# Doublings of the state tables with both parts of a complex number in one instruction

## What is computed

```python
A  = -exp(log_A_real) + 1j * A_imag          # (128 channels, 64 states)
dtA = exp(log_dt)[:, None] * A
Ct = (C_re + 1j * C_im) * (exp(dtA) - 1) / A
V  = exp(dtA[:, :, None] * arange(1024))
K  = 2 * real(einsum('hn,hnl->hl', Ct, V))   # (128, 1024)
y  = irfft(rfft(x, 2048) * rfft(K, 2048))[:1024]
...
gate_logits = xn @ Wg.T; top 2 of 8 experts; softmax over the two
out = sum of gate * (silu(xn @ W1) * (xn @ W2)) @ W3
```

## Time and profile before

| | |
|---|---|
| time of three runs | 861.29 us median (860.84, 861.29, 863.75) |
| profiled execution | span 820.2 us; its own time is not listed apart, and 41.1 us lie between its span and the median of the runs |
| PE busy | 757.8 us (92%), 3893 matmuls |
| DVE busy | 658.9 us (80%) |
| ACT busy | 550.4 us (67%) |
| POOL busy | 146.5 us (18%), 138 instructions |
| 45.9 to 97.8 us of the span | DVE busy 50.2 of 51.9 us, PE 23.7 us, POOL 41.2 us |
| 150 to 820 us of the span | PE busy 658.5 of 670.0 us |

### The profile page before, as it was taken

The page is one execution under the profiler, slowest core; times in us unless marked ns, Lnnn a source line. Parts: engine busy times, 40 slices in busy tenths (PEclk is TensorE's granted clock), DMA queues, the critical chain, the costliest instruction groups (busy, mean ns, idle before and its releaser), DMA issues.

```text
span 820.2 us, 11626 instructions
## 1 busy us (share of the span) xinstructions
PE 757.8 (92%) x3893; PEld 615.2 (75%) x3893; DVE 658.9 (80%) x1558; ACT 550.4 (67%) x939; POOL 146.5 (18%) x138
## 2 busy tenths in 40 slices
PE   6956366999999998999999999999999999999998
PEld 6624255888888645868788878887888887999997
DVE  7699767899937689998799889976777778877775
ACT  5833123344434368898999899889999997665663
POOL 0067775000000254643044000000000000000000
PEclk9978659899999999999999999999999999999999
DMA  8834582689876512413033112211211210000000
GB/s 251 347 104 137 185 285 90 200 250 289 291 223 195 163 40 70 86 54 89 15 102 81 40 38 59 47 43 44 55 45 49 52 27 0 14 14 20 14 20 27
DMA packets 81274, 85.15 MB, mean 104 GB/s; under 512 B 7361, under 2 KB 59841, under 8 KB 80961
## 3 DMA queue, kind: packets, MB, share of 16 engines
q1 hardware_dynamic: 77120, 76.04, 31.3%
q0 software_dynamic: 4096, 8.40, 3.5%
HBM read 59.12 MB, written 25.30 MB: 103 GB/s over the span
## 4 chain that ended last, share of the span: by engine, by line
PE 75%; POOL 9%; DVE 8%; issue 4%; ACT 3%; DMA 1%; SPq 0%; DVEq 0%; POOLq 0%
PE ps L1829 19%; PE ps L1831 18%; PE ps L1830 18%; POOL x_slots L643 9%; PE ps L1948 6%; PE ps L2024 3%; PE ps L2171 3%; DVE hid_lo L1755 2%; PE ps L1842 1%; PE ps L1927 1%; PE ps L2198 1%; PE ps L1869 1%; PE ps L1848 1%; DVE xn L1436 1%; ACT L880 1%
## 5 line engine op out<-in xcount | busy, mean ns | idle before, releaser
L1755 DVE TENSOR_TENSOR hid_lo<-hid,hid_hi 128x512 fp32r<-128x512 f32 x256 | 175.3, 686 | 52.1 <-ACT hid_hi L881 49.5
L880 ACT ACTIVATE hid<-ps,b_sb 128x512 f32<-128x512 f32 x256 | 177.7, 694 | 36.7 <-PE ps L1831 18.8
L881 ACT ACTIVATE hid_hi<-ps,b_sb 128x512 fp32r<-128x512 f32 x256 | 176.0, 688 | 0.0
L1829 PE MATMUL ps<-hid_hi,w_lo 128*128 128x512 f32 x256 | 102.1, 399 | 5.4 <-DVE hid_lo L1755 5.2
L1829 PE MATMUL ps<-xt_hi,w_lo 128*128 128x512 f32 x256 | 102.4, 400 | 1.5 <-DVE xn L1428 1.5
L1831 PE MATMUL ps<-xt_hi,w_hi 128*128 128x512 f32 x256 | 99.9, 390 | 0.0
L1831 PE MATMUL ps<-hid_hi,w_hi 128*128 128x512 f32 x256 | 99.8, 390 | 0.0
L1830 PE MATMUL ps<-xt_lo,w_hi 128*128 128x512 f32 x256 | 99.8, 390 | 0.0
L1830 PE MATMUL ps<-hid_lo,w_hi 128*128 128x512 f32 x256 | 99.8, 390 | 0.0
L792 ACT ACTIVATE act<-ps 128x512 f32<-128x512 f32 (+1 forms) x57 | 34.0, 596 | 81.6 <-PE ps L1831 81.6
L643 POOL DMA_INDIRECT x_slots<-xn,slot x64 | 71.4, 1115 | 62.6 <-DVE expert_of L1158 43.4
(11 more groups left out here) (337 smaller groups left out, 1543.9 us busy)
## 6 DMA issues: line engine op xcount, KB each, us to landing
gate_row<-gates_dram SPq DMA_DIRECT2D x64, 256.0 KB, 4.8
wc<-w_split SPq DMA_DIRECT2D x57, 256.0 KB, 3.7
w_split<-wc SPq DMA_DIRECT2D x8, 768.0 KB, 4.1
x_slots<-prod SPq DMA_DIRECT2D x11, 512.0 KB, 9.7
xc<-x_slots SPq DMA_DIRECT2D x19, 256.0 KB, 4.3
y_slots<-yo SPq DMA_DIRECT2D x19, 256.0 KB, 4.1
wst<-w SPq DMA_DIRECT2D x16, 256.0 KB, 4.7
wd<-w SPq DMA_DIRECT2D x19, 192.0 KB, 3.1
```

The source lines that it names most:

```text
L880: nc.scalar.activation(hid1[:, u % 4], ps[:, u % 4], ACT.Gelu_apprx_tanh, bias=b1_sb[:, u:u + 1])
L881: nc.scalar.activation(hid1_hi[:, u % 4], ps[:, u % 4], ACT.Gelu_apprx_tanh, bias=b1_sb[:, u:u + 1]).then_inc(hid1_done, 1)
L1755: tt(hid1_lo[:, u % 4], hid1[:, u % 4], hid1_hi[:, u % 4].bitcast(F32), sub).then_inc(hid1_lo_done, 1)
L1829: mm(dst, a_lo, b_hi, start=first, stop=False)
```

## The change

Both parts of a complex number are handled in one instruction. The tables' first axis (real, imaginary) becomes part of the shape, so that `here * cosine` is one product of twice the columns, and `here * sines` another, where `sines` takes planes 4 and 6 of `base`, plus and minus the sine (for `high` the other way round, by the negative lags of `turn_lags`). The sum adds the two products crossed: its second input walks the part axis backwards (`at + 3:at + 1:-1`), so that one `add` gives both parts. A level has 6 instructions of 64 x 2^n columns instead of 12 of 32 x 2^n; level 0 is done for `low` as well, instead of two copies. `base_powers` writes the product with the sine to plane 4 and its negative to plane 6. `consts` grows by the ten numbers of `turn_lags`.

```diff
--- before.py
+++ after.py
@@ -137,11 +137,12 @@
         rstd = tmp("rstd", [P, G * B])
         shift0 = tmp("shift0", [P, G * B])
         newton = tmp("newton", [P, G * B])
-        consts = tmp("consts", [P, LO + NB + E + E * E])
+        consts = tmp("consts", [P, LO + 2 * NB + E + E * E])
         count_up = consts[:, 0:LO]
         base_lags = consts[:, LO:LO + NB]
-        rev = consts[:, LO + NB:LO + NB + E]
-        upto = consts[:, LO + NB + E:].rearrange("p (e f) -> p e f", e=E)
+        turn_lags = consts[:, LO + NB:LO + 2 * NB]
+        rev = consts[:, LO + 2 * NB:LO + 2 * NB + E]
+        upto = consts[:, LO + 2 * NB + E:].rearrange("p (e f) -> p e f", e=E)
         wg0_sb = tmp("wg0_sb", [P, E])
         small = tmp("small", [P, 4, HH])
         ks = tmp("ks", [P, 24, HH])
@@ -1181,10 +1182,10 @@
 
                 k = lambda i: base[:, i]
                 col = lambda a: a.unsqueeze(1).broadcast_to((P, NB, HH))
-                lag = base_lags.unsqueeze(2).broadcast_to((P, NB, HH))
+                lag, turn = (a.unsqueeze(2).broadcast_to((P, NB, HH)) for a in (base_lags, turn_lags))
                 tt(k(3), col(AR), lag, mul).then_inc(decay_done, 1)
-                v1 = step.mark(tt(k(0), col(FH), lag, mul))
-                v2 = step.mark(tt(k(2), col(FL), lag, mul))
+                v1 = step.mark(tt(k(0), col(FH), turn, mul))
+                v2 = step.mark(tt(k(2), col(FL), turn, mul))
                 need(v1)
                 v1 = step.mark(ts(k(1), k(0), MAGIC, MAGIC, add, sub))
                 need(v1)
@@ -1201,50 +1202,39 @@
                 k = lambda i: base[:, i]
                 dve.wait_ge(base_done, 4)
                 v1 = step.mark(ts(k(1), k(5), -2.0, 1.0, mul, add))
-                step.mark(tt(k(6), k(3), k(4), mul))
+                v2 = step.mark(tt(k(4), k(3), k(4), mul))
                 need(v1)
-                v1 = step.mark(tt(k(5), k(3), k(1), mul))
-                need(v1)
+                step.mark(tt(k(5), k(3), k(1), mul))
+                need(v2)
+                v2 = step.mark(ts(k(6), k(4), -1.0, None, mul))
+                need(v2)
 
             def doublings(d):
 
                 hs = slice(d * HC, (d + 1) * HC)
-                re, im, g0, g1 = low[:, 0, hs], low[:, 1, hs], high[:, 0, hs], high[:, 1, hs]
+                tables = ((low, 0, 0), (high, NB // 2, 4))
+                step.mark(nc.vector.memset(low[:, 0, hs, 0:1], 1.0))
+                step.mark(nc.vector.memset(low[:, 1, hs, 0:1], 0.0))
+                step.mark(nc.vector.tensor_copy(high[:, 0, hs, 0:1], CTR[:, hs].unsqueeze(2)))
+                v = step.mark(ts(high[:, 1, hs, 0:1], CTI[:, hs].unsqueeze(2), -1.0, None, mul))
                 for n in range(5):
                     a, b_ = slice(0, 1 << n), slice(1 << n, 2 << n)
-                    wide_ = lambda i, v: base[:, v, i, hs].unsqueeze(2).broadcast_to((P, HC, 1 << n))
-                    tmp_ = lambda i: half_way[:, i, :, a]
-                    c, s = wide_(n, 5), wide_(n, 6)
-                    if n == 0:
-                        step.mark(nc.vector.memset(re[:, :, a], 1.0))
-                        step.mark(nc.vector.memset(im[:, :, a], 0.0))
-                        step.mark(nc.vector.tensor_copy(re[:, :, b_], c))
-                        step.mark(nc.vector.tensor_copy(im[:, :, b_], s))
-                        step.mark(nc.vector.tensor_copy(g0[:, :, a], CTR[:, hs].unsqueeze(2)))
-                        v = step.mark(ts(g1[:, :, a], CTI[:, hs].unsqueeze(2), -1.0, None, mul))
+                    need(v)
+                    ready = []
+                    for table, lag_, at in tables:
+                        here = table[:, :, hs, a]
+                        cosine = base[:, 5, lag_ + n, hs].unsqueeze(1).unsqueeze(3).broadcast_to((P, 2, HC, 1 << n))
+                        sines = base[:, 4:7:2, lag_ + n, hs].unsqueeze(3).broadcast_to((P, 2, HC, 1 << n))
+                        step.mark(tt(half_way[:, at:at + 2, :, a], here, cosine, mul))
+                        ready.append(step.mark(tt(half_way[:, at + 2:at + 4, :, a], here, sines, mul)))
+                    for (table, lag_, at), v in zip(tables, ready):
                         need(v)
-                    else:
-                        step.mark(tt(tmp_(0), re[:, :, a], c, mul))
-                        step.mark(tt(tmp_(1), im[:, :, a], s, mul))
-                        step.mark(tt(tmp_(2), re[:, :, a], s, mul))
-                        v_low = step.mark(tt(tmp_(3), im[:, :, a], c, mul))
-                    c, s = wide_(n + 5, 5), wide_(n + 5, 6)
-                    step.mark(tt(tmp_(4), g0[:, :, a], c, mul))
-                    step.mark(tt(tmp_(5), g1[:, :, a], s, mul))
-                    step.mark(tt(tmp_(6), g1[:, :, a], c, mul))
-                    v_high = step.mark(tt(tmp_(7), g0[:, :, a], s, mul))
-                    if n:
-                        need(v_low)
-                        step.mark(tt(re[:, :, b_], tmp_(0), tmp_(1), sub))
-                        step.mark(tt(im[:, :, b_], tmp_(2), tmp_(3), add))
-                    need(v_high)
-                    v = step.mark(tt(g0[:, :, b_], tmp_(4), tmp_(5), add))
-                    if n < 4:
-                        v = step.mark(tt(g1[:, :, b_], tmp_(6), tmp_(7), sub))
-                        need(v)
-                    else:
-                        need(v)
-                        tt(g1[:, :, b_], tmp_(6), tmp_(7), sub).then_inc(tables_done, 1)
+                        crossed = half_way[:, at + 3:at + 1:-1, :, a]
+                        op = tt(table[:, :, hs, b_], half_way[:, at:at + 2, :, a], crossed, add)
+                        if table is high and n == 4:
+                            op.then_inc(tables_done, 1)
+                        else:
+                            v = step.mark(op)
 
             angles()
             w0_low(0)
@@ -2242,6 +2232,7 @@
     dft = np.stack([np.cos(angle), -np.sin(angle)]).astype(np.float32)
     fwd = dft.reshape(2, CT, P, HF).transpose(2, 1, 0, 3)
     inv = dft.transpose(0, 2, 1).reshape(2, HM, P, C).transpose(2, 1, 0, 3)
+    lags = 2 ** np.array([1, 2, 3, 4, 5, 8, 0, 9, 6, 7])
     tile, expert = np.divmod(np.arange(T * E), E)
     earlier = (tile[:, None] < tile) & (expert[:, None] == expert)
     prefix = np.concatenate([earlier, expert[:, None] == np.arange(E)], 1).astype(np.float32)
@@ -2256,7 +2247,7 @@
             np.concatenate([a["L0_ffn_W3"].transpose(0, 2, 1), np.broadcast_to(a["L0_attn_ln_b"], (E, 1, H)),
                             np.zeros((E, J0 * P - HID0 - 1, H), np.float32)], 1)
             .reshape(E, J0, P, P).transpose(0, 2, 1, 3).reshape(E, P, J0 * P)], 2),
-        lag_row=np.concatenate([np.arange(LO), 2 ** np.array([1, 2, 3, 4, 5, 8, 0, 9, 6, 7]), E - np.arange(E), np.tril(np.ones((E, E))).ravel()]).astype(np.float32),
+        lag_row=np.concatenate([np.arange(LO), lags, np.where(np.arange(NB) < NB // 2, lags, -lags), E - np.arange(E), np.tril(np.ones((E, E))).ravel()]).astype(np.float32),
         prefix=prefix.reshape(2, P, T * E + E).transpose(1, 0, 2),
         dft_fwd=fwd, dft_inv=inv,
         wqk_t=np.stack([a["L1_attn_W_query"].T, a["L1_attn_W_key"].T], 1),
```

## The result

The changed kernel took 851.07 us in the median of four runs (849.2 to 851.92), the kernel before 861.15 beside it: a ratio of 0.9847, 95% interval 0.981 to 0.9884, so some 10 us or 1.5% faster. The forecast was 864.3, within 861.8 to 866.4.

What follows compares the result with a forecast made beforehand. PE's start of chunk 1 was taken as bound by the later of two paths: DVE, 3.6 us earlier, and scatters, last one 4.7 us later. Net +3.0 us on 861.3 gave 864.3 us, range 861.8 to 866.4.

Steps and rivals of the forecast that it cites:

- Net 3.6 us earlier: DVE's doublings: fewer instructions, less one added scaling, end 3.6 us earlier (3.0 to 4.0).
- I take nothing: DVE's crossed sums: the backward step of the second input costs no extra time per column.
- its rival: DVE's crossed sums are slow: up to 8 us more, 866 to 869 us in all; chance 0.05.
- Scatters are held longer: POOL's scatters beside wider DVE instructions: holds of 9.2 us instead of 5.3, last scatter 4.7 us later.
- 1.0 us: Last doubling level: a scatter waits this long for a 1024-column DVE instruction's end, twice in each half.
- the first rival: Longer DVE instructions do not hold scatters longer: 859.6 us, or 857.7 if scatters were even freed; chance 0.10.
- the 0.6 on entering the last level: POOL's scatters: 0.6 us of hold in each half where the doublings' last level begins.
- the spectra's products: DVE products of 512 columns beside the last half dozen scatters: 0 to 1.7 us more hold, 0.8 taken.
- the runs' median stands 41.1 above the span, so 861.3 + 3.0: Whole kernel: 41.1 us added to the forecast span of 823.2 us, giving 864.3 us.
- two paths meet at the start of chunk 1's up products: PE's start at 144.46 awaits the later of the scatter path (142.80) and the DVE path, 1.66 us later.
- not named: Something unnamed in DMA traffic that comes 3.6 us earlier, either side; chance 0.05.
- the case that I described: Chunk 1's up products: DVE path ends at 140.9, scatter path at 147.5, so PE starts 3.0 us later.

Runs made afterwards that it cites:

- a_again: The changed kernel run and profiled again with no edit: 849.09 us, ratio 0.986 to the kernel before.
- b_again: The kernel before run and profiled again with no edit: 861.24 us, profiled span 863.4 us.
- after: The changed kernel as first measured and profiled: 851.07 us, profiled span 847.4 us.
- a_spaced: The changed kernel with a POOL memset of 256 columns ahead of each scatter from scatter 20 on: 840.87 us.
- b_spaced: The kernel before with a POOL memset of 256 columns ahead of each scatter from scatter 20 on: 840.5 us.
- b_hold: The kernel before with a POOL memset of 256 columns ahead of every second scatter from 8 to 30: 856.38 us.
- the pads: The changed kernel with unused products behind each half of the doublings: three of 512 columns (856.97 us) or one (857.13 us).
- a_lead: The changed kernel with one of two products of the last level left out: 854.22 us.
- b_lead: The kernel before with three of eight products of the last level left out in each half: 861.6 us.

## Why the prediction was wrong

**"Net 3.6 us earlier" on DVE: right in kind, 0.7 too much.** The subtraction of the fifth expert came 2.92 us earlier. Halves of the doublings last 15.62 and 15.63 us instead of 17.31 and 17.25, the scaling costs 0.39. Levels 1, 2 and 4 saved what was counted; level 0 saved nothing (1.47 us for 1.43, where I had 1.29), for its instructions of 64 columns start 0.17 apart, not 0.13 as those of level 1 in the earlier trace rows; and level 3 saved 0.30, where 0.42 was counted. "I take nothing" for the backward step was right, so its rival fell.

**Scatters are held longer: right; their sum and their tail were mis-sized.** They took 1.96 us beside 1024 columns, twice in each half, where 0.96 and "1.0 us" of waiting were worked out. The Trainium skill's rule that the shared read interface is held for the whole instruction (SBUF — State Buffer, Who interferes with whom) agrees with this, the remark on the same page that tensor_tensor did not stall such DMAs doesn't, and with it the first rival fell. But the holds in the two halves came to 7.4 us (scatters 10 to 34), not 9.2: beside the level of 512 columns, where 0.9 was counted for each half, 0.1 and 0.4 came, and the 0.6 on entering the last level came in one half only. Scatter 35 came 2.1 us later, not 3.9 (3.5 in `a_again` against `b_again`, both from their first scatter), and the last one 1.2, not 4.7 (2.2 in that pair). From scatter 38 on all of the changed kernel's take 0.96 us, where four of before take 1.29 to 1.55: the spectra's products, counted with 0.8 more, came only after the last scatter.

**The sum: its base failed.** The step that failed first is "the runs' median stands 41.1 above the span, so 861.3 + 3.0": it took 41.1 as a constant around the span. In `b_again` the profiled execution took 865.25 us with a span of 863.4, so that term is 2 us; the time of the execution shown is not on record. The others lie within the span of usual executions and were absent from the one shown: 32.5 ahead of chunk 1's up products (144.46 to 176.95) and 10.8 behind them (675.7 to 686.5). That "two paths meet at the start of chunk 1's up products" was true of an execution like none of the runs on record (the fastest of before took 845.98, this one's span is 820.2). In the others the stalled stretch decides which of PE's steps wait: in `after` chunk 1's up products start at 162.85, 18.4 us later than in the execution shown and 14.1 earlier than in `b_again`. There what I booked as the cost, scatters held longer, goes with the gain. What was "not named" had 0.05.

**Where its mechanism holds.** With the stretch all but closed, `a_spaced` against `b_spaced` is the case that I described: DVE's subtraction 2.5 us earlier (93.55 for 96.09), the last scatter 2.3 later, and chunk 1's up products with it, 2.4 later (157.64 for 155.27), not +3.0. The medians differ by 0.4 us. There the change is worth nothing; its 10 to 12 us are what it takes off the stretch, and a memset ahead of each scatter takes off more.

**Open.** Shown is that the stretch needs scatters under way, ends in a pause of theirs, opens earliest where they were held least ahead of it, and hardly opens with POOL instructions between them. What in the chip stalls, why in steps of 0.70 us, and what tips it over at a given moment, no run shows. Full DMA engines are not what keeps it up: their share is 0.29 from 120 to 130 us of the changed kernel, against 0.79 in the 10 us before. That the change gains by its hold is argued from the order of the runs and not shown, for no run holds scatters without parting them or moving DVE. Nor does hold alone explain the changed kernel: `b_hold` and the pads delay scatter 36 as much (102.5 to 102.7), and stay at 856 to 857, since ACT's first copy is due 1 to 5 us later there (113.2 to 115.4) and is caught. Part of it is chance: a kernel's runs lie at several levels (before 845.98 to 869.58, `a_lead` 847.36 to 854.36), and each has one profile here. A bare wait between scatters, without a memset, wasn't tried, and nor was the loading of instructions, which passes DMA queues of its own (q8 and q14 on the page). And whether SP's loads and stores of weights, which run when stretches open, have a part in it wasn't tried.

## What to carry to other kernels

Set the profiled execution's span against the median of the runs before building on it: of 41 us between them all but 2 were no overhead but waits that this execution had not met, and in `b_again` one stall alone made 32.5. Several engines idle at once, released from "remote" in the profile, beside a long row of indirect DMAs on POOL, are such a stall; a small POOL instruction between the scatters is a cheap test, and here it was the better change (840.5 against 851.07). What an edit does to the rhythm of such a row can outweigh what it saves on its own engine.

## What the runs showed of the hardware that I had not expected

- While indirect DMAs follow each other at 1.26 us, the other engines can fall into starts 0.70 us or multiples of it apart, with signals many us late (ACT's second copy into `half_way` waits 16.08 us in `after`, 2.65 in `b_spaced`), for some 30 us (`after`) to 50 us (`b_lead`); POOL doesn't slow down.
- A memset of 64 columns on POOL (0.17 us) fills the gap of 0.30 between two scatters, costs 0.03 us of pace, and khat, stalled until 129 without it, ran at 116.
- A DVE instruction on 1024 columns holds a scatter to 1.96 us, one on 512 to 1.50.
